# A graph network's plain aggregation: rows fetched by two more engines, and who writes zeros into a PSUM bank

## What is computed

```python
# L2, twice
agg = jax.ops.segment_sum(h[src] * norm[:, None], dst, num_segments=n)
# L3, once
msg_sum = jax.ops.segment_sum(hn[src], dst, num_segments=n)
```

## Time and profile before

| what | us |
|---|---|
| median of 3 runs | 20450.03 (20449.54 to 20452.8) |
| span of the profiled execution | 20464.9 |
| aggregation 1, first to last of L851 | 11955.5 to 14732.3 |
| aggregation 2 | 14815.7 to 17591.5 |
| aggregation 3 | 17744.5 to 20424.2 |

### The profile page before, as it was taken

The page is one execution under the profiler, slowest core; times in us unless marked ns, Lnnn a source line. Parts: engine busy times, 40 slices in busy tenths (PEclk is TensorE's granted clock), DMA queues, the critical chain, the costliest instruction groups (busy, mean ns, idle before and its releaser), DMA issues. The chain is left out here.

```text
span 20464.9 us, 176272 instructions
## 1 busy us (share of the span) xinstructions
PE 7887.3 (39%) x37282; PEld 6279.5 (31%) x37282; DVE 6583.0 (32%) x14435; ACT 1536.0 (8%) x3978; POOL 11444.9 (56%) x12037
## 2 busy tenths in 40 slices
PE   2222222222233333365655543343443334334444
PEld 1222222222221111255555532232332223223323
DVE  4444443444443333233333331121221112322112
ACT  3000000000001000122222210000000000100000
POOL 4666655666646666654544545565465556356555
PEclk5555555555655555688888865555555555555555
DMA  5222213111111111222222321111111111111111
GB/s 136 52 52 52 52 46 57 44 44 44 44 38 20 25 27 23 43 70 69 70 68 69 70 62 37 37 46 38 56 47 37 38 37 47 37 38 47 41 39 49
DMA packets 1319746, 996.38 MB, mean 49 GB/s; under 512 B 759983, under 2 KB 1141132, under 8 KB 1316902
## 3 DMA queue, kind: packets, MB, share of 16 engines
q0 software_dynamic: 384896, 686.86, 13.0%
q1 hardware_dynamic: 703358, 276.09, 5.8%
q10 hardware_dynamic: 230728, 25.44, 0.9%
HBM read 868.48 MB, written 132.38 MB: 49 GB/s over the span
## 5 line engine op out<-in xcount | busy, mean ns | idle before, releaser
L851 POOL DMA_INDIRECT wk<-tab,srcT x4912 | 4638.0, 944 | 3767.2 <-issue 1421.9
L970 POOL DMA_INDIRECT hs<-tab_g,srcT x3328 | 3150.4, 947 | 1884.2 <-issue 948.3
L885 PE MATMUL PS<-wk 128*128 128x128 f32 x9888 | 2520.7, 434 | 3593.1 <-DMA wk<-tab,srcT 3329.1
L885 PEld LDWEIGHTS PS<-wk 128*128 128x128 f32 x9888 | 2159.7, 322 | 4216.3 <-DMA wk<-tab,srcT 3895.9
L919 DVE TENSOR_TENSOR F<-F,PS 128x512 f32 x1248 | 856.2, 686 | 6647.8 <-remote 3684.5
L1910 POOL DMA_INDIRECT wk<-tab,hs x1776 | 1679.0, 945 | 1706.4 <-DMA hs<-rec_d 1140.6
L1830 POOL DMA_INDIRECT rec_d<-hs x1664 | 1619.4, 973 | 832.0 <-issue 523.0
L1161 DVE TENSOR_TENSOR F<-F,PS 128x126 f32 x3328 | 950.5, 286 | 2570.4 <-ACT hs L1060 1127.5
L1117 PE MATMUL PS<-wk,hs 128*128 128x128 f32 x6656 | 1272.9, 369 | 741.5 <-DVE hs L1146 576.4
L1117 PEld LDWEIGHTS PS<-wk,hs 128*128 128x128 f32 x6656 | 1183.2, 275 | 833.2 <-issue 774.3
L1097 PE MATMUL PS<-ident,wk 128*128 128x128 f32 (+1 forms) x104 | 45.1, 434 | 2253.6 <-ACT wk L1041 2145.0
(11 more groups left out here) (400 smaller groups left out, 11220.6 us busy)
## 6 DMA issues: line engine op xcount, KB each, us to landing
hs<-tab_b SPq DMA_DIRECT2D x1776, 56.0 KB
own_rows<-tab SPq DMA_DIRECT2D x6144, 0.5 KB
wk<-tab,srcT POOLq DMA_INDIRECT x4912
wk<-tab ACTq DMA_DIRECT2D x4096, 0.5 KB
hs<-tab_g,srcT POOLq DMA_INDIRECT x3328
wk<-tab,hs POOLq DMA_INDIRECT x1776
rec_d<-hs POOLq DMA_INDIRECT x1664
rec_d<-F SPq DMA_DIRECT2D x1, 15984.0 KB
```

The costliest lines, as they stand in the source:

```text
L851: pool.indirect_dma_start(gbuf[m % 4 * QUAD + u], None, table, bass.IndirectOffsetOnAxis(srcT[:, edges_of(k)], 0))\
L885: last = pe.matmul(to, rows[u], onehot[j], start=False, stop=u == QUAD - 1, skip_group_check=True)
L970: pool.indirect_dma_start(gt[n % 2][:, j, :], None, table, bass.IndirectOffsetOnAxis(srcT[:, n * BT + j:n * BT + j + 1], 0)).then_inc(half ...
```

## The change

No quad is fetched row by row any more: POOL gathers all 416 in each of the three calls, 1,664 indirect DMAs instead of 1,632 (first two) and 1,648 (third). The loops of SP and ACT, their two buffers and their semaphores are gone. PE's product of zeros is gone too: ACT copies a tile of zeros from SBUF (now 128 x 512 floats) into the bank as soon as DVE has read it (`added`), up to 6 quads ahead, and signals `bank_clear`; PE waits for that and for the rows. In the third call ACT's copies of the own rows stand in the same program, between the clears.

```diff
-        def fetch_rows(eng, kind, table, first, buf, nums, nums_sig, row_sigs):
...
-        def aggregate(number, table, loading=(), pe_beside=None, dve_beside=None, act_program=None, last_load=None):
+        def aggregate(table, loading=(), pe_beside=None, dve_beside=None, act_beside=None, last_load=None):
...
-                    fetch_rows(sp, mybir.EngineType.SP, table, ROW_SP, own_rows[:, :], own_nums[:, :], nums_in, row_in[number])
                     if last_load is not None:
                         last_load(sp)
...
-                    for m, g in enumerate(by_tile):
-                        if m % 2 == 0 and m >= 4:
-                            pool.wait_ge(summed.sem, summed.after(by_tile[m - 3] + 1))
+                    for g in range(NQD):
+                        if g % 2 == 0 and g >= 4:
+                            pool.wait_ge(summed.sem, summed.after(g - 2))
...
-                        if g >= NBK:
-                            pe.wait_ge(added.sem, added.after(g - NBK + 1))
-                        if g == 0:
-                            pe.wait_ge(onehot_ready.sem, onehot_ready.after(1))
-                        pe.matmul(bank(g % NBK), zeros[:, 0:P], zeros, start=True, stop=False, skip_group_check=True)
-                        if g in by_sp:
...
+                        pe.wait_ge(bank_clear.sem, bank_clear.after(g + 1))
+                        pe.wait_ge(gathered[g % 4].sem, gathered[g % 4].after((g // 4 + 1) * 16 * QUAD))
+                        rows = gbuf[g % 4 * QUAD:(g % 4 + 1) * QUAD]
...
+                @block.scalar
+                def _(act):
+                    act.wait_ge(onehot_ready.sem, onehot_ready.after(1))
+                    for g in range(NQD):
+                        if act_beside is not None:
+                            act_beside(act, g)
+                        if g >= NBK:
+                            act.wait_ge(added.sem, added.after(g - NBK + 1))
+                        act.copy(bank(g % NBK), zeros).then_inc(bank_clear.sem, 1)
...
-        def own_rows_act(act):
-
-            for c in range(NCH):
+        def own_rows_act(act, g):
+
+            c = step_of(g, 2)
+            if c is not None:
                 act.wait_ge(pe_a.sem, pe_a.after(c + 1))
                 act.wait_ge(pe_b.sem, pe_b.after(c))
```

More of the change, by code:

```diff
@@ L60 @@
 LR = 8
-RPER, RNUM = 100, 4
-ROW_SP, ROW_ACT = 94, 99
 NT_B = (KT + P - 1) // P
@@ L151, in build @@
         sm = sb("sm", [P, 4 * NT])
-        own_rows = sb("own_rows", [P, RQ * P])
-        own_nums = sb("own_nums", [1, RQ * P], I32)
         PS = ctx.enter_context(nc.psum_tensor("PS", [P, 8 * 512], F32))
@@ L203, in build @@
         idx_taken = sig("idx_taken")
[L204 to L207, removed]
         order_in = sig("order_in")
+        bank_clear = sig("bank_clear")
         spread = sig("spread", 0)
@@ L804, in edges_of @@
             return slice(c, c + 1)
-        def fetch_rows(eng, kind, table, first, buf, nums, nums_sig, row_sigs):
[L808 to L824, removed]
-        def aggregate(number, table, loading=(), pe_beside=None, dve_beside=None, act_program=None, last_load=None):
+        def aggregate(table, loading=(), pe_beside=None, dve_beside=None, act_beside=None, last_load=None):
             NH, NQD, NBK, W4 = K // HALF, K // QUAD, 6, QUAD * P
[L829 to L832, removed]
+            zeros = wk[:, 4 * HALF * P:4 * HALF * P + W4]
             with nc.Block() as block:
@@ L924, in aggregate @@
             for a, s in enumerate(gathered[0:4]):
[L925 to L928, removed]
+                s.passed(16 * QUAD * (NQD // 4))
             summed.passed(NQD)
             added.passed(NQD)
+            bank_clear.passed(NQD)
             onehot_ready.passed(NH)
@@ L2234, in build @@
         columns = lambda n: [(bcol[:, m:m + 1], colv(t["L2_gnn_" + name + n])) for m, name in enumerate(("b", "g", "be"))]
-        aggregate(0, tab, loading=columns("1") + [(W[0], t["L2_gnn_W1"]), (W[1], t["L2_gnn_W2"])],
+        aggregate(tab, loading=columns("1") + [(W[0], t["L2_gnn_W1"]), (W[1], t["L2_gnn_W2"])],
                   pe_beside=turn_own_rows, dve_beside=add_own_rows, last_load=bring_dinv)
@@ L2249, in add_bias @@
                 v.tensor_tensor(xg, xg, every(bias_ps), ALU.add)
-        aggregate(1, tab, loading=columns("2") + [(W[0], t["L2_gnn_Wf"]), (bias_b[0], row(t["L2_gnn_bf"]).broadcast_to([P, D]))],
+        aggregate(tab, loading=columns("2") + [(W[0], t["L2_gnn_Wf"]), (bias_b[0], row(t["L2_gnn_bf"]).broadcast_to([P, D]))],
                   dve_beside=add_bias)
@@ L2402, in own_rows_dve @@
                 v.tensor_tensor(xc, xc, extra_ps[:, 0:len(tiles_in(c)) * P], ALU.add).then_inc(dve_a.sem, 1)
-        aggregate(2, tab, loading=[(W[0], t["L3_gnn_W_self"]), (W[1], t["L3_gnn_W_neigh"]),
+        aggregate(tab, loading=[(W[0], t["L3_gnn_W_self"]), (W[1], t["L3_gnn_W_neigh"]),
                                 (bias_b[0], row(t["L3_gnn_b"]).broadcast_to([P, D])),
                                 (gamma, colv(t["L3_gnn_gamma"])), (beta, colv(t["L3_gnn_beta"]))],
-                  pe_beside=own_rows_pe, dve_beside=own_rows_dve, act_program=own_rows_act)
+                  pe_beside=own_rows_pe, dve_beside=own_rows_dve, act_beside=own_rows_act)
         pe_a.passed(NCH); pe_b.passed(NCH); pe_c.passed(1); act_a.passed(NCH); dve_a.passed(NG + NCH); dve_b.passed(3)
```

4 lines of the change are left out of this document (2 added, 2 removed).

## The result

The changed kernel takes **19298.79 us** (median of 4 runs, 19284.76 to 19317.66). The kernel before took 20451.42 us beside it (median of 4, 20449.54 to 20473.17). The ratio is 0.9436, 95% interval 0.9423 to 0.9450. The forecast was 19285 us in a range of 18980 to 19530. The profiled execution took 19304.66 us, with a span of 19302.8 us; the sum had given 19300.4 us for it.

The account below looks back on a forecast made before the run. POOL's gathers were held by SP's late single rows and short pauses for PE's signals. The span of 20464.9 us less 1164.5 gave 19300.4, less 14.9 to the median 19285 us; range 18980 to 19530.

Parts of the forecast that it names:

- the sum: Profiled span before, 20464.9 us, less the 1164.5 us forecast for the aggregations: a span of 19300.4 us.
- Steps 1 and 2: Aggregations: all 12 stalls go with the single rows; POOL issues 80 more gathers, 32, 32 and 16 by stage.
- Step 3, the rhythm: Aggregations: 24 gathers in 34.00 us make 2355.9 us a stage, 7067.8 in all against 8232.3: -1164.5 us.
- the lower end: Aggregations: POOL pauses only every 8 quads, 44.0 us per 32 gathers, 2287 us a stage: -1371 us, 19079 us.
- Steps 4 and 5: PE's product of zeros was covered by waits, ACT's copy of zeros (taken as 0.59 us) is hidden: 0 each.
- Step 6: Third aggregation: 25 clears behind ACT's wait for PE's transposes, taken as 0, upper bound +108 us.
- The last step, from the span to the median: Whole kernel: the profiled span is 14.9 us over the runs' median, so 19300.4 us becomes 19285 us.
- Step 7: SP's load of `dinv` starts earlier in stage 1: 0; the wider fill of zeros costs under 1 us.
- the clock: PE already runs at 1.2 GHz nearly all the time; less work could add up to 4 us.
- The rival of no short pauses: Aggregations: POOL never stops, 2079 us a stage, -1996 us, 18454 us in all; chance 0.09.
- The evidence from the attention layer: Without a product of zeros, ACT gets PE's signal 13.5 us late and POOL still pauses 4.30 us.
- The slower side: Aggregations: without the zero product POOL stops at every second quad, +511 us, 20961 us; chance 0.05.

Follow-up runs that it names:

- e1: Kernel before without the singly fetched rows, PE's product of zeros kept, on the chip where the kernel before takes 20454.67 us: 19313.61 us, ratio 0.9442.
- e9: Changed kernel, unedited, on a chip where the kernel before takes 15951.26 us: 16047.69 us, ratio 1.0061.
- e5: Changed kernel with row buffers for six quads instead of four, on the chip where the kernel before takes 20454.67 us: 19288.89 us, ratio 0.9431.
- e12: Kernel before, unedited, run for its trace on the chip where its median is 15951.26 us: 15947.34 us in its one run.
- e7: Changed kernel with a waited-for memset before each gather, on a chip where the kernel before takes 15973.5 us: 16525.72 us, ratio 1.0346.
- e8: Changed kernel gathering half of each row, on a chip where the kernel before takes 15973.5 us: 16072.41 us, ratio 1.0062.

## Why the prediction was right

- **Steps 1 and 2, the single rows and their 80 gathers: right on chip A.** The stalls were the late rows (e1), and POOL's own chain is what remains. The twelve stalls were 1232.5 us; 80 more gathers at 1.42 us take back 113, and the rest, some 47 us, is the pauses coming at 24 gathers throughout. What I didn't see was that the worth of this step hangs on how fast a single row goes out beside gathers: 1.68 us gave a stall, 0.53 us gives none. The prediction's 1.29 us held for the interval between rounds, but only because the stall itself sped the rows up. Without a stall only step 2 is left, 80 x 1.25 = 100 us on the slow side, and e9 shows 96.
- **Step 3, the rhythm: right.** 2355.9 us a stage were forecast from 24 gathers in 34.00 us; 2354.9, 2354.7 and 2356.7 came. The pause put off to every 8 quads, the lower end, came in e5, but not with the pause of 4.33 us that the end assumed: it grew to 5.6 us, and the time stayed. That end of the range was mis-sized: with 32 gathers between pauses the first stage got 5 us shorter (2350.2 against 2354.9), not 69.
- **Steps 4 and 5, the zeros: right.** e1 puts the move of the zeros at some 15 us, within what can't be told from nothing, and at 1.7 us within the stages. ACT's copy takes 589 ns, as the 0.59 taken.
- **Step 6, the third aggregation: 0 was right,** of a span of 0 to 108. PE's waits for the clears in the stage with own rows, after the change:

```profile
PE PS L840 <- ACT PS L853: 37.2, 16, 3.9
```

The first two stages have 4 and 3 such waits, so these are the own-row steps, as the step said might come: at 17389.06 ACT copies the own rows, and PE's next quad, at 17391.37, waits for the clear. But it waits 2.34 us there, and quads that wait for their gather wait some 2.9, so nothing is lost. The stage is 2 us longer than the others, and so is e1's (2357.2 against 2355.8 and 2355.0), where ACT clears nothing: the 2 us aren't the clears either.
- **The last step, from the span to the median, is most of the miss.** The span was forecast 2.4 us too low (19300.4 against 19302.8). The 14.9 us between span and median were carried over from the kernel before; for the changed kernel they are 4.0 (19302.8 - 19298.79). So near a hit also took luck: the spread of the runs alone is 33 us.
- **Step 7 and the clock: nothing seen.** From 12700 to 13000 us the granted clock was 0.51 before and is 0.50 after: the low level, 1.2 GHz, in both. The 4 us that the Trainium skill's rule would add are too few to be seen in the time.
- **The rival of no short pauses** (18454 us) is not what chip A did. But its length of a stage, 1663 x 1.25 = 2079 us, is what e9 has, 2079.5, 2075.9 and 2075.8. There the rule of the Trainium skill that I set against the rows ("PSUM — Partial Sum Buffer", "Engine vs sequencer instructions"), that an increment fires when its matmul completes, agrees with the trace to 0.13 us; on chip A it does so right after a pause, and is up to 15.5 us off later. These rows show when the waiting engine acts, and no run shows when the increment itself was sent.
- **The evidence from the attention layer was misread, in the rival's favour.** ACT's copy at 4027.55 belongs to the first of the two quads in that row of 16 matmuls. That of the last one, which ends at 4014.01, is this:

```profile
4034.59 0.17 ACT L1060 COPY hs<-PS 128x8 f32<-128x8 f32 x1 [6.87 <-remote]
```

So the signal of the last product came 20.6 us late, not 13.5. The argument against the rival holds the more. On chip C (e12) all 832 of these copies start within 0.04 us.
- **The slower side** had 0.05, from bunches that come closer. That did not happen: the changed kernel and e1 have no two pauses less than 24 gathers apart. On chips B and C every kernel with fewer single rows, or none, is slower than the kernel before, by a way I had not priced: that there may be no stall to remove. The prediction gave no chance to another chip, and that the result fell on one like that of the trace before is the condition for its being right.

## What to carry to other kernels

When a helper queue is to relieve the bounding engine, compare its round with the stretch of work that it hides behind, at the pace it has *beside* that work: not alone, and not averaged over the stall that it causes. 512 rows at 1.68 us against 577 us of quads turned 100 us of help into 1232 us of stalls. A short pause that recurs is read by its rate over a long run: where a deeper buffer makes the pauses rarer and longer in step, as in e5, it buys nothing. And a gain that comes from removing a stall is only as general as the stall: time such a change on more than one chip before it is kept, since here its sign differs between chips.

## What the runs showed of the hardware that was not expected

**The same kernel takes 20454.67 us on one chip and 15973.5 or 15951.26 on two others.** The engines' own work is nearly the same. The part ahead of the aggregations, which the change doesn't touch, in the changed kernel on chip A (length, then busy PE, PEld, DVE, ACT and POOL, granted clock, DMA share, GB/s):

```profile
0.00:11945.00 11945.00, 4496.40 (x24910) 3798.34 (x24910) 4790.15 (x12006) 1428.38 (x3767) 6792.33 (x7124) 0.65 0.24 53
```

and on chip C (e9):

```profile
0.00:9529.00 9529.00, 4125.48 (x24910) 3443.60 (x24910) 4776.62 (x12006) 1447.80 (x3767) 6801.78 (x7124) 0.68 0.31 67
```

The same 7,124 instructions on POOL are busy for 6792 and 6802 us, those on DVE for 4790 and 4777; PE is 8% less busy on chip C. So the 2416 us between the two lengths are nearly all waits. In the attention layer's gathers, for one, 1886.2 us of idle time on chip A are 1021.3 on chip C.

What chip A's traces have in common is that other parties are held up while POOL issues indirect gathers: PE's signals are acted on up to 10.5 us late in nine quads of ten, or up to 22.4 with six quads in flight; a row DMA of SP takes 1.68 us instead of 0.53; both catch up when POOL stops. The run length and the pause go together so that a gather costs 1.41 or 1.42 us on average, against 1.25 on chips B and C. Whether it is bytes, descriptors or semaphore updates that are worked off in the pause was to be told by e7 and e8 and was not, as they and their repeats ran on chips without the effect. Nor do the runs tell whether it belongs to chip A for good or to its condition at the time.
